# A 5x5 convolution computed two neighbouring pixels at a time: seven products of tap vectors in place of ten

## The reference

```python
def _L0_conv_ref(x, w3, b3, w5, b5, wr, br):
    y3 = conv(x, w3, 'SAME') + b3;  y5 = conv(x, w5, 'SAME') + b5
    P = jnp.pad(y3, ((0, 0), (0, 0), (1, 1), (1, 1)))
    shifts = [P[:, :, 2 - sw:2 - sw + H, 2 - sh:2 - sh + W] for sh in range(3) for sw in range(3)]
    stacked = jnp.stack([y5] + shifts, axis=2)
    return jnp.einsum('bcghw,cg->bchw', stacked, wr[:, :, 0, 0]) + br[None, :, None, None]
def _L1_conv_ref(x, filters):     # 3x3 patches with a 1 in front, all products of two entries
    feat = (spot[..., :, None] * spot[..., None, :]).reshape(spot.shape[:-1] + (M * M,))
    return jnp.einsum('bcyxf,ocf->boyx', feat, filters.reshape(O, C, M * M))
x = x + _L0_conv_ref(_gn(x), ...)
x = x + _L1_conv_ref(_gn(x), L1_conv_filters)
```

## Time and profile before

| what | value |
| --- | --- |
| median of 3 runs | 337.11 us (337.1 to 337.4) |
| profiled execution | 337.04 us |
| its span (first to last instruction or transfer) | 335.2 us |
| busy share PE / DVE / ACT / POOL | 94% / 54% / 24% / 3% |
| mean granted TensorE clock | 0.994 of full |
| first matmul of the first stage | 17.91 us |
| first matmul of the second stage | 114.51 us |

### The profile page before, as it was taken

One profiled execution on the slowest core, in us unless ns is written; L12 is line 12 of the kernel. 1 busy time (PEld: TensorE's weight loads), 2 busy tenths in 40 slices (PEclk: granted clock), 3 DMA queues, 4 the chain that ended last, 5 costly groups with the idle time before them and its releaser, 6 DMA issues.

```text
span 335.2 us, 15654 instructions
## 1 busy us (share of the span) xinstructions
PE 314.7 (94%) x7560; PEld 163.4 (49%) x7560; DVE 181.0 (54%) x215; ACT 82.0 (24%) x135; POOL 11.3 (3%) x34
## 2 busy tenths in 40 slices
PE   0689999999999999999999999999999999999990
PEld 0234674344764436444736464644734564645550
DVE  2869783045597246022896955367005298883031
ACT  3610380070690254100000021783000000000091
POOL 3540000000000000000000000000000000000000
PEclk9999999999999999999999999999999999999997
DMA  6944000000000000000000000254000000000047
GB/s 201 367 100 103 4 4 2 2 5 2 4 4 4 2 3 4 4 2 2 4 2 4 4 4 2 53 111 96 4 2 2 4 4 2 4 4 2 4 98 157
DMA packets 7630, 11.59 MB, mean 35 GB/s; under 512 B 5392, under 2 KB 5520, under 8 KB 7440
## 3 DMA queue, kind: packets, MB, share of 16 engines
q1 hardware_dynamic: 5104, 9.59, 10.6%
q10 hardware_dynamic: 2464, 1.01, 1.3%
HBM read 6.40 MB, written 4.19 MB: 32 GB/s over the span
## 4 chain that ended last, share of the span: by engine, by line
PE 92%; DVE 3%; DMA 2%; SPq 1%; DVEq 0%; issue 0%
PE acc L631 91%; DMA raw<-in_x 2%; DVE stats L498 1%; PE acc L679 1%; PE acc L657 1%; DVE plane L516 1%; SPq L233 0%; DVE product L556 0%; SPq L237 0%; PE acc L667 0%; DVEq L81 0%; DVE norm L513 0%; SPq L226 0%; DVE mean_var L504 0%; DVE norm L510 0%
## 5 line engine op out<-in xcount | busy, mean ns | idle before, releaser
L631 PE MATMUL acc<-product,weight 32*32 32x512 f32 (+1 forms) x4416 | 182.5, 597 | 0.0
L584 DVE TENSOR_TENSOR product<-plane 128x4096 f32<-128x4096 f32 x24 | 105.1, 4424 | 63.9 <-PE acc L631 63.9
L631 PEld LDWEIGHTS acc<-product,weight 32*32 32x32 f32 (+1 forms) x4416 | 96.2, 111 | 82.2 <-issue 58.8
L631 PE MATMUL acc<-plane,weight 32*64 32x512 f32 (+1 forms) x2048 | 102.0, 595 | 0.8 <-DVE plane L516 0.8
L631 PEld LDWEIGHTS acc<-plane,weight 32*64 32x64 f32 (+1 forms) x2048 | 45.1, 119 | 49.6 <-issue 43.6
L328 ACT ACTIVATE raw<-acc,offset_by_strip 32x512 f32<-32x512 f32 x36 | 24.4, 679 | 99.6 <-PE acc L631 99.1
L631 PE MATMUL acc<-plane,middle 32*64 32x512 f32 (+1 forms) x640 | 38.2, 593 | 0.0
L326 ACT ACTIVATE raw<-acc 32x512 f32<-32x512 f32 x48 | 28.2, 587 | 32.0 <-PE acc L631 31.4
L547 DVE COPY raw<-acc 32x512 f32<-32x512 f32 x16 | 11.1, 694 | 24.7 <-PE acc L631 24.3
L355 ACT ACTIVATE product<-plane 128x4096 f32<-128x4096 f32 x2 | 7.3, 3634 | 63.2 <-PE acc L631 63.1
L631 PEld LDWEIGHTS acc<-plane,middle 32*64 32x64 f32 (+1 forms) x640 | 15.6, 119 | 14.5 <-issue 12.8
(11 more groups left out here) (70 smaller groups left out, 61.8 us busy)
## 6 DMA issues: line engine op xcount, KB each, us to landing
raw<-in_x SPq DMA_DIRECT2D x8, 512.0 KB, 8.4
out<-raw SPq DMA_DIRECT2D x12, 256.0 KB, 3.0
filters_in<-in_L_conv_filters SPq DMA_DIRECT2D x4, 400.0 KB, 3.9
out<-product SPq DMA_DIRECT2D x8, 64.0 KB, 2.4
out<-product ACTq DMA_DIRECT2D x8, 64.0 KB, 2.7
w_in<-in_L_conv_w ACTq DMA_DIRECT2D x4, 100.0 KB, 3.6
w_in<-in_L_conv_w ACTq DMA_DIRECT2D x2, 36.0 KB, 1.8
w_in<-in_L_conv_w SPq DMA_DIRECT2D x2, 36.0 KB, 2.2
```

The lines of the kernel that those rows point to most:

```text
L584: nc.vector.tensor_tensor(product_rows(n), inner(g, 0, H), shifted(g, PRODUCTS[k]), ALU.mult)\
L631: return nc.tensor.matmul(acc[32 * s:32 * (s + strips), h, r, :], weights[32 * r:32 * r + 32, t:t + strips, :] .rearrange("p t c -> p (t c ...
```

## The change

**Arithmetic.** Two horizontal neighbours, an even pixel and the odd one beside it, are computed together. Write p(k) for the pixel at distance k from the even one, and a, b, c, d, e for the tap columns at -2 to 2. The ten column products become seven, each over half as many columns of pixels and all rows, so that 512 pixels of a matmul now cover the strip of a whole group: `total`, p(-1)+p(0), with (a+b+c)/2; `step`, p(0)-p(-1), with (a-b+c)/2; `next`, p(2), with d+e; `left`, p(-2)-p(0), with a; `step after`, the same differences one pair further on, with -d; `right`, p(1)-p(-1), with c; `far`, p(3)-p(2), with e. The even pixels are whole + cross + (left, step after); the odd ones whole - cross + (right, far), where whole is `total` + `next` and cross is `step`.

**What computes what.** `halve` (DVE) makes five half-width images per group from `plane[g]`, reading every second pixel: four into the product buffers, `far` into `scaled3`, whose shifts have been used by then. PE accumulates whole in `acc[:, 0]` and cross in `acc[:, 1]`. ACT copies whole to `even_half` (`keep_whole`). `whole_and_cross` (DVE) makes the difference (`odd_half`) and the sum (`even_half`) from it and `acc[:, 1]`. `odd_half` of group 0 lies in `filters_in`, so this waits until the filters have been read (`sums_ready`). PE meanwhile accumulates left and step after in `acc[:, 0]`, later right and far in `acc[:, 1]`; `finish_even` and `finish_odd` (DVE) add these. ACT alone then writes the pixels to `raw[g]`, every second one (`spread`, 16 instructions for the even and 16 for the odd pixels of a group); the 48 copies of ACT and 16 of DVE in the first stage go.

**Moves.** The filter additions and the edge taps move from DVE to POOL; the zero borders of the four product buffers are set by POOL after the first stage. Row edges get products of their own, as the column edges had: `edges0` issues 80 matmuls of 64 pixels and 16 of one pixel per group, all on the four diagonal tiles; that of group 0 stands within the first products of group 1, that of group 1 within the second stage. The order of the shifts (`EY_EX`) is turned so that the tap columns d and e are complete after six additions. The constant term of the filters is summed by DVE (`add_constants`) in place of a small matmul. The second stage is otherwise unchanged. The diff, cut to its core:

```diff
-COLUMNS0 = (-2, -1, 1, 2, 0)
-EY_EX = [(ey, ex) for ex in (-1, 0, 1) for ey in (-1, 0, 1)]
...
+HALVES = {"total": (-1, 0, HALF_W), "step": (0, -1, HALF_W + 1), "left": (-2, 0, HALF_W),
+          "right": (1, -1, HALF_W), "far": (3, 2, HALF_W)}
+SECOND_AT = LINES * HALF_W
...
+EY_EX = [(ey, ex) for ex in (1, 0, -1) for ey in (-1, 0, 1)]
...
+PAIR_AT = TAPS0
+EDGE_AT = PAIR_AT + 5
...
-            for n in range(PRODUCT_BUFS):
-                borders_of(product[n], PROD_AT, PROD_USED).then_inc(borders, 1)
...
+            for g in range(NG):
+                for name in ("total", "step", "left", "right"):
+                    pad_half(g, name).then_inc(padded, 1)
...
-                if n < len(EY_EX) - 1:
-                    pool.wait_ge(shift_folded, n + 1)
+                pool.wait_ge(shift_folded, n + 1)
+                if n == 5:
+                    nc.gpsimd.tensor_tensor(folded[:, PAIR_AT:PAIR_AT + 5, :], folded[:, 15:20, :], folded[:, 20:25, :],
+                                            ALU.add).then_inc(columns_added, 1)
...
+            nc.gpsimd.memset(folded[:, EDGE_AT:N_WEIGHT0, :], 0.0).then_inc(edges_folded, 1)
+            pool.wait_ge(edges_folded, 1)
...
+                    last = nc.gpsimd.tensor_tensor(part, part, row, ALU.subtract)
+                last.then_inc(edges_folded, 1)
+                pool.wait_ge(edges_folded, e + 3)
...
+            pad_half(0, "far").then_inc(far_padded, 1)
+
+
+            pool.wait_ge(filters_landed, 16 * GROUP)
+            for y in range(3):
+                nc.gpsimd.tensor_tensor(sums[:, y:9:3, :], filt[:, 1 + 3 * y:4 + 3 * y, :],
+                                        filt[:, M * (1 + 3 * y):M * (4 + 3 * y):M, :], ALU.add)
...
+            last.then_inc(sums_ready, 1)
...
+            for n in range(PRODUCT_BUFS):
+                g = n // 2
+                pool.wait_ge(part_done, 4 * (g + 1))
+                if n == 1:
+                    pool.wait_ge(odd_spread, GROUP * NG)
+                else:
+                    pool.wait_ge(even_spread, GROUP * (g + 1))
+                borders_of(product[n], PROD_AT, PROD_USED).then_inc(borders, 1)
...
+            def keep_whole(g):
+                act.wait_ge(part_done, 4 * g + 1)
+                nc.scalar.activation(even_half(g), part_acc(0), ACT.Copy).then_inc(kept, 1)
+
+            def spread(g, odd, images):
+
+                half = odd_half(g) if odd else even_half(g)
+                act.wait_ge(odd_ready if odd else even_ready, g + 1)
+                for r in images:
+                    for s in range(STRIPS):
+                        y = SIDE_ROWS * (s // 2) + 1 - s % 2
+                        to = raw[g][32 * r:32 * r + 32, :].rearrange("p (y x) -> p y x", x=W)
+                        last = nc.scalar.activation(to[:, y:y + SIDE_ROWS - 1:2, odd:odd + W - 1:2],
+                                                    half[32 * s:32 * s + 32, CHUNK * r:CHUNK * r + CHUNK]
+                                                    .rearrange("p (y x) -> p y x", x=HALF_W), ACT.Copy)
+                    last.then_inc(odd_spread if odd else even_spread, 1)
...
+            keep_whole(0)
             std(1)
             normalise(1)
-            copy_columns(0)
-            evict(0)
-            evict(1)
-            copy_columns(1)
+            spread(0, 0, range(GROUP))
+            copy_edges(0)
+            spread(0, 1, (0, 1))
+            keep_whole(1)
+            spread(0, 1, (2, 3))
             std(2)
             normalise(2)
             square(0)
-            evict(2)
-            evict(3)
+            spread(1, 0, (0, 1))
+            copy_edges(1)
+            spread(1, 0, (2, 3))
+            spread(1, 1, range(GROUP))
...
+            def halve(g, name):
+
+                one, other, width = HALVES[name]
...
+                nc.vector.tensor_tensor(lines(buf, at, pitch)[:, 2:2 + H, 0:width], every_second(one), every_second(other),
+                                        ALU.add if name == "total" else ALU.subtract)\
+                    .then_inc(half_ready[g][name], 1)
+
+            def outer_taps():
+                dve.wait_ge(shift_folded, len(EY_EX))
+                step(turn(0, TAPS0))
...
+            def whole_and_cross(g):
+                dve.wait_ge(kept, g + 1)
+                dve.wait_ge(part_done, 4 * g + 2)
+                if g == 0:
+                    dve.wait_ge(sums_ready, 1)
+                step(nc.vector.tensor_tensor(odd_half(g), even_half(g), part_acc(1), ALU.subtract))
+                nc.vector.tensor_tensor(even_half(g), even_half(g), part_acc(1), ALU.add).then_inc(whole_cross_ready, 1)
+
+            def finish_even(g):
+                dve.wait_ge(whole_cross_ready, g + 1)
+                dve.wait_ge(part_done, 4 * g + 3)
+                nc.vector.tensor_tensor(even_half(g), even_half(g), part_acc(0), ALU.add).then_inc(even_ready, 1)
+
+            def finish_odd(g):
+                dve.wait_ge(part_done, 4 * g + 4)
+                nc.vector.tensor_tensor(odd_half(g), odd_half(g), part_acc(1), ALU.add).then_inc(odd_ready, 1)
...
-            fold_edges()
+            dve.wait_ge(padded, 4 * NG)
+            halve(0, "total")
+            outer_taps()
+            middle_taps(0)
+            halve(0, "step")
+            halve(0, "left")
+            halve(0, "right")
             make_ring()
+            turn_edges()
+            dve.wait_ge(far_padded, 1)
+            halve(0, "far")
+            add_constants()
+            whole_and_cross(0)
             last = statistics(1, wait_piece(1), every)
+            finish_even(0)
             normalise(1, last)
-            evict(0)
-            fold_filters()
-            evict(1)
+            middle_taps(1)
+            halve(1, "total")
+            halve(1, "step")
+            finish_odd(0)
+            halve(1, "left")
+            turn_filters()
+            halve(1, "right")
+            halve(1, "far")
+            whole_and_cross(1)
             finish_x1(0)
-            normalise(2, statistics(0, lambda n: None, every))
+            last = statistics(0, lambda n: None, every)
+            finish_even(1)
+            normalise(2, last)
+            finish_odd(1)
             for k in range(1, PRODUCT_BUFS):
                 multiply(0, k)
...
+            def column0(odd, stack, at, pitch, x0, every, five, start, stop, pairs):
+
+                def tile(r, s, strips, d, t, first_one, last_one):
+                    y = SIDE_ROWS * (s // 2) + d + 2
+                    pixels = lines(stack, at, pitch)[32 * r:32 * r + 32, y:y + SIDE_ROWS - 1:2,
+                                                     x0:x0 + every * (HALF_W - 1) + 1:every]
+                    return nc.tensor.matmul(acc[32 * s:32 * (s + strips), odd, r, :],
+                                            five[32 * r:32 * r + 32, t:t + strips, :].rearrange("p t c -> p (t c)"),
+                                            pixels, start=first_one, stop=last_one, tile_position=(32 * r, 32 * s))
...
+                source, x0 = ("step", 1) if name == "step after" else (name, 0)
+                five = {"total": middle0[g][:, 1, :, :], "step": middle0[g][:, 2, :, :], "left": weight0[:, 0:5, :],
+                        "step after": minus_one, "right": middle0[g][:, 0, :, :], "far": weight0[:, 20:25, :]}[name]
+                pe.wait_ge(half_ready[g][source], 1)
+                pe.wait_ge(outer_ready, 1)
+                pe.wait_ge(middle_ready, g + 1)
+                return column0(odd, *half_at(g, source), x0, 1, five, start, stop, pairs)
+
...
+            def edges0(g):
+
+                pe.wait_ge(edge_ready, 1)
+                pe.wait_ge(odd_ready, g + 1)
+                for t in range(-2, 3):
+                    for side in range(4):
+                        first = PLANE_AT + (0, (H - 1) * PITCH, 0, W - 1)[side] + t * (1, 1, PITCH, PITCH)[side]
+                        for r in range(GROUP):
+                            if side < 2:
+                                pixels = plane[g][32 * r:32 * r + 32, first:first + W]
+                            else:
+                                pixels = plane[g][32 * r:32 * r + 32, first:first + (H - 1) * PITCH + 1:PITCH]
+                            nc.tensor.matmul(acc[32 * r:32 * r + 32, 1, side, 0:W],
+                                             weight0[32 * r:32 * r + 32, EDGE_AT + 5 * side + t + 2, :], pixels,
...
+            PAIRS_FIRST, SINGLES_FIRST = (True, False), (False, True)
+
+            def rest0(g, forms):
+
+                part(g, ("step",), 1, forms)
+                pe.wait_ge(kept, g + 1)
+                part(g, ("left", "step after"), 0, forms[::-1])
+                pe.wait_ge(whole_cross_ready, g + 1)
+                part(g, ("right", "far"), 1, forms)
+
+            pe.wait_ge(plane_dve, 1)
+            pe.wait_ge(plane_act, 1)
+            product0(0, "next", 0, True, False, True)
+            product0(0, "next", 0, False, False, False)
```

(18 more changed lines are left out.)

386 lines of the change are left out of this document (185 added, 201 removed).

## The result

The changed kernel takes 333.82 us (median of 4 runs, 333.14 to 334.67) against 337.22 us for the kernel before, measured beside it: a ratio of 0.9903, 95% interval 0.9879 to 0.9927, so it is about 1% shorter, 3.4 us: little, but beyond the interval. Forecast were 332.1 us, range 324 to 342. The profiled execution took 334.25 us for a span of 332.5, 2.7 us less than the 335.2 before; forecast was 5.0 less.

The account below looks back on a forecast made before the run. PE was taken to bound the kernel: 25.3 us less work against 18.9 us of new waits. Span 335.2 - 6.7 + 1.7 for the clock = 330.2, plus 1.84 around it: 332.1 us, range 324 to 342.

Parts of the forecast that it names:

- Rival A: Whole kernel: the case as worked out, 332.1 us, own range 328 to 337; chance 0.52.
- S: Time when POOL's filter sums are ready and DVE's combinations may start: 45.6 us; the change gains while below 50.6.
- B: Rival: POOL not held up by DVE's additions and multiplications, sums ready at 36 to 40, 324.7 us; chance 0.16.
- D: Rival: DVE's reads of every second pixel cost 2.1 ns, each image 1.7 us or more dearer, 344 us; chance 0.08.
- C: Rival: POOL's stepped reads cost three times contiguous ones, each small instruction 0.14 us; S 55.9, time 342.2 us; chance 0.17.
- E: Rival: ACT's `spread` takes 0.8 us instead of 0.645, 5 us on the way to buffer 1, 337 us; chance 0.07.
- The start: First stage's beginning: a tenth POOL addition for the d+e taps makes PE begin 0.85 us later.
- POOL's price for the sums: 27 filter additions on POOL: 3.6 ns an element for 1,728 elements plus 0.04 us fixed each, 6.9 us.
- The DVE chain: DVE's work from S to the edges of group 0, nothing beside it: 24.0 us, edges starting at 69.8.
- From the edges to the second stage: PE's edges 4.0, two pairs forms 7.0, cross 4.5, two double products 18.0: second stage starts at 103.3 us.
- The clock: PE's granted clock falls while PE mostly waits, from 59.5 to 69.8 us: price 1.7 us, ends 0 and 3.5.
- The last wait: Second stage: the fourth multiplication ends 0.5 us after PE wants it.

Follow-up runs that it names:

- experiment 1: Changed kernel with the odd half of group 0 in a buffer of its own, no wait for the filter sums: 324.86 us, ratio 0.963 to the kernel before.
- experiment 3: Changed kernel with four of the five images of group 0 made by transposes with one SBUF operand: 329.02 us, ratio 0.975 to the kernel before.
- experiment 9: Kernel of experiment 7 with the odd half of group 1 in `filters_in`, so POOL clears buffers 1 and 2 without waiting for `spread`: 320.55 us.
- experiment 4: Changed kernel with 24 zero-weight matmuls added on PE in the wait before the edges of group 0: 333.21 us, ratio 0.9876 to the kernel before.
- experiment 5: Changed kernel with `next` reading neighbouring pixels instead of every second one: 333.1 us in one run.
- experiment 7: Kernel of experiment 1 with both forms of `next` of group 1 ahead of `total`, and `finish_odd(0)` before image `step`: 320.58 us, ratio 0.9501.
- experiment 8: Changed kernel with only the new order of experiment 7, the wait for the filter sums kept: 327.94 us, ratio 0.972 to the kernel before.

## Why the prediction was right, and by how much its terms were off

Rival A, the case that was forecast, is what happened. The place and the order of the five waits that came, the two falls of the clock, and POOL as the head of the chain were as worked out. The number says less: the range, 324 to 342, held a loss as well as a gain, and of the forecast 5.0 us of span 2.7 came. That the error stayed at 2.3 us is in part luck, since terms that were too low (the sums, the edges, `next`) met others that were too high (DVE's chain, the clock, the last wait). S went one for one into the end (experiment 1). B is out, since experiments 3 and 1 show the exclusion; D is out with 2.28 us an image. C named the right mis-sized quantity, the small instruction's fixed part, but its reads at three times the contiguous ones were wrong. E's sign is there, `spread` at 0.68 us a copy instead of 0.645 and buffer 1 freed at 132.66, but PE did not wait for it, since the second stage began later too; and experiment 9, in the reordered kernel, shows that an earlier buffer gives nothing. The second stage began 3.8 us later than forecast. By terms:

- **The start.** PE's first product began at 19.43, not at 17.91 + 0.85 = 18.76. POOL's additions began 0.7 us later in this trace (12.02, before 11.34), and the tenth, forecast as one of 0.80, took 1.65 beside DVE's plane instruction. None of it reached the end: the middle taps were ready at 27.2 instead of 26.9, and the sums began at the forecast 36.5.
- **POOL's price for the sums** is the step that was mis-sized. "0.04 fixed remains" was read from memsets, which overlap one another. The 27 instructions tell it directly (min/median/max in ns):

```profile
L385 POOL TENSOR_TENSOR sums<-filters_in x21: 300/416/545, 41.0 to 47.9; 128x32 f32<-128x32 f32 x9, 128x64 f32<-128x64 f32 x9, 128x96 f32<-128x96 f32 x3
L372 POOL TENSOR_TENSOR sums<-filters_in x3: 540/543/2626, 36.5 to 37.5; 128x96 f32<-128x96 f32 x3
```

  0.30 us for 32 elements and 0.54 for 96: (0.54 - 0.30)/64 = 3.8 ns an element and 0.18 fixed. These additions, too, overlap one another by 0.04: the 21 of them take 7.27 us where their durations add up to 8.15. So 0.14 fixed remains, the figure of rival C, where 3.6 and 0.04 were taken. 27 instructions, 1,728 elements and three copies (0.36 instead of 0.54) come to 9.7 us by that, and 9.7 is what the sums took without the one hold-up of 2.1, not 6.9. So S came at 48.2 and not 45.6. (The forecast's own terms give 6.7, not the 6.9 written there.) Rival C's factor of three for the reads was 3.8 / 2.2 = 1.7, with (0.39 - 0.25)/64 = 2.2 ns an element for the contiguous additions above.
- **The DVE chain** from S took 23.3 us, not 24.0, 0.7 us back. In part that is its four additions with an operand in PSUM, which take 2.27 to 2.29 us, as those in SBUF do, not 2.35. (In the forecast 45.6 + 24.0 is 69.6, not the 69.8 written there.)
- **From the edges to the second stage** 35.4 us, not 33.5. Edges and corners took 5.0 instead of 4.0: 0.65 of it is the clock, and 0.36 a price set too low, since at the full clock they took 4.36 (experiment 4). The pairs form of `next` took 3.96 to the next product, not 3.48: 9% for its step, where "I take 0" stood within ends of 0 and 2.7, and 0.14 for the clock. The other 0.4 lies spread over the products behind.
- **The clock** was put at 1.7 us. The first fall costs nothing: the pairs form of `right` took 5.44 us where that of group 1, at the full clock, took 3.63, and the wait into which that went, forecast at 1.8, is gone. Experiment 1 agrees: there this fall did not happen, and the kernel gained 9.0 us, for the 8.9 by which DVE began earlier, and not 1.8 more. The second costs 0.8 (0.65 and 0.14). So some 0.9 less than forecast.
- **The last wait** of 0.5, for the fourth multiplication, did not come either.

The sum, made as the prediction made its own: the second stage begins at 107.1, `edges0(1)` takes 4.6 to the next product, no wait comes behind it: an equivalent of 111.7, against 107.8 and 1.7 for the clock, 109.5. That is 2.2 us more than forecast, and the span, 332.5, is 2.3 above 330.2. The median of the time lies 1.7 above 332.1; it is 0.4 below the profiled execution.

Of the two rules that the prediction took from the Trainium skill, the first held here and the second held for DVE alone. By the Trainium skill, page "SBUF — State Buffer", section "Who interferes with whom", the second of the two instructions is blocked for the whole of the first. Single additions of 2.50 to 2.93 us, 2.1 above the undisturbed ones, beside DVE additions of 2.29 agree, and so do experiments 3 and 1, where with one operand in SBUF no addition is held up like that. By the same page of the Trainium skill, section "Door 1: The DMA port swizzle", a step of two float32 is free. DVE's 2.28 us for 2,048 elements with that step, against 4.42 for 4,096 neighbouring ones, agree. For PE's reading the trace does not: it costs 8 to 9% (experiment 5).

So where did the arithmetic's gain go? Of the 25.3 us of matmuls saved, 22.5 came back by the second stage (111.7 against 114.51). PE's first product began 1.5 us later, and behind it PE waited 14.8 us; with the first, for the taps, the five waits add up to 16.4. The other 6.2 us PE worked longer than forecast: 2.6 by the lowered clock, 0.8 by the step of `next`, 1.0 by edges dearer than 4.0; 1.8 are left, which no run takes apart. Half of the waits have one cause: in experiment 1 they add up to 8.2. And 9.0 us of the whole time (experiment 1) are owed to one borrowed buffer: through it the filter sums, work for which nobody had waited, came onto the first stage's only chain. Two calls in an unlucky order take another 4 to 6 (experiments 7 and 8). In experiment 7, with both mended, 3.0 us of waits are left in place of 16.4.

## What to carry to other kernels

When a busy engine's work is cut by passing its results through another, list what that second engine must have done before, and whose buffer it writes: here a borrowed buffer alone cost 9 us, and giving it up together with two moved calls won 13. Price small instructions from small instructions of the same kind, not from the slope of large ones or the distance of memsets. An engine that is off the path in the old profile (POOL at 3%) has no known price for what is moved to it, so work out the latest time at which the result is still free, as the 50.6 us here, and see how far the forecast is from it.

## What the runs showed of the hardware

- A POOL addition of 96 elements takes 0.39 us with contiguous operands and 0.54 with operands that step by 400 bytes; 32 elements 0.25 and 0.30. The fixed part is 0.18 us; the stepped ones overlap one another by 0.04 of it. DVE needs 0.34 and 0.24 for the same stepped reads the earlier trace rows.
- A DVE addition of 2.29 us with both operands in SBUF held up POOL's additions by 2.1 us; one with an operand in PSUM held up none (7.27 us for the same 21 beside it and alone), nor did a transposition (4.77 us for twelve, against 10.86).
- PE reading every second float32 is 8 to 9% slower (0.47 against 0.43 to 0.44 us for eight matmuls).
- Eighty products of 64 pixels take 3.85 us on the four diagonal tiles and 2.38 spread over all sixteen (2.31 at a granted clock of 0.50), but the one-pixel products behind the spread ones started only after a pause of 1.5 to 1.9 us. Unexplained.
- PE idle from about 46 to 53 us saw its granted clock fall to 0.50 by 50 us, and it was back at full after some 3.5 us of matmuls. This fall cost nothing, as another wait of PE followed; the one before the edges, with work behind it, cost 0.8 us.
